# Attention scores as float32 products in four row groups of packed keys, in place of two bfloat16 products over split operands

## The chip, the cores and the metric

The kernel runs on one core of one Trainium2 chip. The metric is the time of one launch in microseconds of the device (us); the lower the better. Engines: TensorE (PE: matmuls, PEld: loading of its stationary operand), VectorE (DVE), ScalarE (ACT), GpSimd (POOL) and SyncE (SP, which only issues DMAs).

## What is computed

Four blocks act on x of (2 images, 32 channels, 64 x 64 pixels) in float32, each as x = x + block(normalised x). Three are convolutions: two deformable 3x3 convolutions with a 1x1 one between them. The fourth is attention over the N = 4096 pixels of each image, and the change is there:

```
f1 = einsum('oc,bcn->bon', w1, g) + b1      # queries, 32 channels
f2 = einsum('oc,bcn->bon', w2, g) + b2      # keys
f3 = einsum('oc,bcn->bon', w3, g) + b3      # values
A  = softmax(einsum('bcn,bcm->bnm', f1, f2), axis=-1)
x  = x + (einsum('bcm,bnm->bcn', f3, A) + g)      # g: x normalised for each channel
```

## The kernel before, in words

Every engine has its own program of instructions, executed in the order in which they are written; semaphores order the engines among each other. There is no scheduler: the order in the source is the order on the chip. So an instruction that waits holds up all that is queued behind it on its engine.

The last convolution samples by four corners. Image 0 is finished first: a part of it by products of whole bands of rows (`dense_and_tiles`), the rest, like all of image 1, by tiles of 128 pixels, whose corners POOL fetches with nine indirect DMAs a tile (L499) into four slots. A slot is free when the tile four before it has been sampled. For one tile VectorE weights the corners (L818) and adds them (L828, L832), TensorE turns the samples (`turn`, L1656), ScalarE copies them out (`tile`, L1337), TensorE multiplies them by the weights (`convolve`, L1664), and VectorE adds the result to x (`finish`, L853). Image 1 has 32 tiles: eight go through in `pairs(1, ...)`, between the band work and attention, in four pairs with attention's preparation beside them; the other 24 go through beside the attention of image 0, four in each of its first six blocks (the merged blocks).

Attention goes over 8 blocks of 512 queries for each image (`attend`), and for each block over 16 pairs of 128 keys (step s). Three things are done for a block:

- **Maxima of the next block.** 32 products of 128 queries by 512 keys from the high bfloat16 parts alone (`score_chunks`, L1808, "chunks"), written to two PSUM banks in turn; VectorE takes each one's maximum along the row (`largest`, L1085). Chunk c may be written when the maximum of chunk c-2 has been taken. At the block's end the maxima are negated, split in three bfloat16 parts (`negated`, L1092 to L1101), turned on TensorE (`turn_maxima`, L1816) and copied into a row (`maxima_row`, L1109).
- **Scores.** Queries and keys stand as three bfloat16 parts (high, middle, low). A pair of key tiles takes two products of 128 rows (L1851) and two of 67 rows, which hold the rest and the maxima's row (L1855). They go to two of four banks, so that ScalarE's exponential (L1455, 1024 wide) of one pair runs beside the next pair's scores.
- **Weighted sums.** Values times probabilities (`weigh`, L1826) in float32, two products of 64 columns in one bank. ScalarE copies the block's sums out (L1447), VectorE adds both halves, divides and adds to x (`sum_part` k = 0 to 6).

Ahead of it, for each image: projections (`project`, L1762) in float32, ScalarE's high parts (L1409, L1410), VectorE's remainders (`split`, L1031 to L1034), 32 turns of the values (L1782) and twelve DMAs by SP that spread the parts over the partitions (`spread_a`, `spread_b`). For image 1 all of this stands in the last two blocks of image 0 (`prepare_image_1`). The number of chunks in each step, and the steps of the sum's parts, come from tables:

```
CHUNKS = [2] * 8 + [3] * 4 + [2] * 2 + [0] * 2
MERGED_CHUNKS = [2, 2, 3, 3, 1, 2, 3, 3, 1, 2, 3, 3, 2, 2, 0, 0]
LAST_CHUNKS = [0] * 7 + [4] * 8 + [0]
```

In a merged block a tile takes four steps: its corners are weighted at s % 4 == 0, summed at s % 4 == 1, turned at the end of s % 4 == 2 and convolved at the end of s % 4 == 3.

## Time and profile before

| | |
|---|---|
| median of 3 runs | 1409.59 us (1409.26 to 1412.25) |
| the profiled execution | 1411.1 us, of which its span is 1409.0 us |
| busy, share of the span | TensorE 85%, VectorE 73%, ScalarE 45%, GpSimd 38% |
| chain that ended last | TensorE 62%, VectorE 22%, issue 8%, DMA 3%, ScalarE 2% |
| TensorE's granted clock, mean | 0.927 of full |

The stages by time (us from the span's start): up to 250 the first convolution, to 300 the 1x1 one, to 601 the second convolution's bands with the tiles of image 0, 601 to 691 `pairs(1, ...)`, 691 to 969 the six merged blocks, 969 to 1085 the two blocks in which image 1 is prepared, 1085 to 1398 image 1's attention, then its last sum and the store.

Busy times of engines are read beside each other within one stage. A row of the timeline gives a start, a duration, an engine, a line of the kernel and the tiles written and read; a count "x4" means that so many instructions in a row were merged. A float32 product is recorded as two instructions.

### The profile page before, as it was taken

What the parts mean: (1) busy time and instruction counts of PE and PEld (TensorE: products, weight loads), DVE (VectorE), ACT (ScalarE), POOL (GpSimd) and SP (SyncE); (2) the same over time, 40 slices, a digit from 0 to 9 for tenths busy, and PEclk for the clock granted to TensorE, in tenths of its full rate; (3) what the DMA queues carried; (4) which work ended last, traced back from release to release, by engine and by line L of the source; (5) the groups of instructions that cost most, each with busy time, mean ns of one, the idle gap of its engine ahead of it and who ended that gap; (6) DMA issues with size and microseconds to landing.
All of it is one profiled execution on the core that took longest, in us unless ns stands there. A gap on an engine that the chain in (4) does not pass through costs nothing.

```text
span 1409.0 us, 18575 instructions
## 1 busy us (share of the span) xinstructions
PE 1201.2 (85%) x6192; PEld 484.6 (34%) x6253; DVE 1031.7 (73%) x1727; ACT 636.5 (45%) x772; POOL 541.7 (38%) x530
## 2 busy tenths in 40 slices
PE   3688883287999999965799999998888999999996
PEld 0466662042444444322233333332222222222221
DVE  5399998874866666576779888988757677777771
ACT  2666665345455545240144444344562444444443
POOL 8000000247787877776777777760000000000000
PEclk9899997598999999955699999999998999999998
DMA  1455540047433352115111111110021000000000
GB/s 42 105 121 115 123 106 1 0 136 248 147 112 114 113 151 73 49 53 129 51 51 51 51 50 52 50 41 0 0 60 31 15 0 1 0 0 0 0 0 15
DMA packets 59201, 86.58 MB, mean 61 GB/s; under 512 B 12358, under 2 KB 39494, under 8 KB 58246
## 3 DMA queue, kind: packets, MB, share of 16 engines
q1 hardware_dynamic: 44166, 55.09, 15.1%
q0 software_dynamic: 14976, 30.70, 7.7%
q8 instruction: 37, 0.61, 0.2%
q14 instruction: 22, 0.18, 0.0%
HBM read 72.12 MB, written 7.34 MB: 56 GB/s over the span
## 4 chain that ended last, share of the span: by engine, by line
PE 62%; DVE 22%; issue 8%; DMA 3%; ACT 2%; DVEq 1%; SPq 1%; another core or an unknown queue 1%; ACTq 0%
PE psum L1692 16%; PE psum L1826 14%; PE psum L1808 8%; PE psum L1851 6%; PE psum L1855 6%; DVE maxes L1085 4%; PE psum L1664 3%; DVE products_or_attention L699 3%; PE psum L1702 2%; DVE probs_and_weighted L699 2%; PE psum L1529 2%; DVE probs_and_weighted L828 1%; PE psum L1656 1%; DVE quads L341 1%; DVE probs_and_weighted L818 1%
## 5 line engine op out<-in xcount | busy, mean ns | idle before, releaser
L499 POOL DMA_INDIRECT tile_data<-quad_table,index_u x468 | 493.2, 1054 | 160.8 <-issue 142.0
L1085 DVE TENSOR_REDUCE maxes<-psum 128x1 f32<-128x512 f32 x512 | 337.9, 683 | 128.9 <-PE psum L1808 113.8
L1455 ACT ACTIVATE probs_and_weighted<-psum 128x1024 f32<-128x1024 f32 x256 | 262.1, 1024 | 355.9 <-PE psum L1855 355.6
L1826 PE MATMUL psum<-probs_and_weighted,quads 128*64 128x512 f32 x1024 | 280.6, 627 | 0.5
L1692 PE MATMUL psum<-scratch,quad_rows_or_splits 128*128 128x512 f32 x486 | 227.5, 609 | 12.6 <-DVE scratch L914 12.6
L1855 PE MATMUL psum<-products_or_attention 67*128 (+1 forms) x512 | 155.2, 384 | 1.1 <-DVE products_or_attention L1109 1.1
L1692 PEld LDWEIGHTS psum<-scratch,quad_rows_or_splits 128*128 128x128 f32 x486 | 88.1, 192 | 125.9 <-issue 125.9
L341 POOL TENSOR_SCALAR quads<-x_state,norm 32x4096 f32<-32x4096 f32 x6 | 34.1, 5679 | 235.7 <-DVE norm L583 234.9
L925 DVE TENSOR_TENSOR probs_and_weighted<-psum,quads 128x512 f32<-128x512 f32 x81 | 55.3, 687 | 90.6 <-PE psum L1692 85.0
L1808 PE MATMUL psum<-products_or_attention 128*128 128x512 bf16 x250 | 101.9, 419 | 17.8 <-DVE maxes L1085 15.0
L1581 PE MATMUL psum<-quad_rows_or_splits 64*128 64x128 f32 x1152 | 83.6, 288 | 26.3 <-DVE products_or_attention L699 18.2
L1808 PE MATMUL psum<-tile_data 128*128 128x512 bf16 x246 | 91.1, 392 | 6.7 <-DMA tile_data<-quad_rows_or_splits 4.6
L1337 ACT ACTIVATE vals<-psum 96x384 f32<-96x384 f32 x52 | 25.3, 486 | 140.7 <-PE psum L1656 140.7
L1826 PEld LDWEIGHTS psum<-probs_and_weighted,quads 128*64 128x64 f32 x1024 | 51.2, 136 | 103.2 <-issue 100.0
L1581 PEld LDWEIGHTS psum<-quad_rows_or_splits 64*128 64x128 f32 x1152 | 72.6, 193 | 39.4 <-ACT quad_rows_or_splits L1304 22.7
L1363 ACT ACTIVATE quads<-quads,band_columns 128x512 f32<-128x512 f32 x81 | 52.5, 711 | 65.6 <-DVE probs_and_weighted L925 65.6
L1851 PE MATMUL psum<-tile_data 128*128 (+1 forms) x236 | 72.9, 384 | 7.4 <-DMA products_or_attention<-quad_rows_or_splits 4.7
L1851 PE MATMUL psum<-products_or_attention 128*128 (+1 forms) x231 | 72.6, 388 | 4.0 <-issue 4.0
L1855 PEld LDWEIGHTS psum<-products_or_attention 67*128 67x128 bf16 x512 | 50.7, 99 | 63.8 <-issue 2.8
L818 DVE TENSOR_TENSOR probs_and_weighted<-tile_data 128x1152 f32<-128x1152 f32 x52 | 70.3, 1351 | 0.0
L1529 PE MATMUL psum<-quads,off_w 128*32 128x512 f32 x256 | 33.3, 666 | 41.4 <-DVE quads L341 41.4
L1808 PEld LDWEIGHTS psum<-products_or_attention 128*128 (+1 forms) x256 | 23.5, 97 | 123.8 <-DVE maxes L1085 61.5
(204 smaller groups left out, 1402.6 us busy)
## 6 DMA issues: line engine op xcount, KB each, us to landing
products_or_attention<-positions SPq DMA_DIRECT2D x32, 576.0 KB, 8.3
products_or_attention<-bands SPq DMA_DIRECT2D x18, 768.0 KB, 9.9
tile_data<-quad_table,index_u POOLq DMA_INDIRECT x468, 2.5
quads<-bands SPq DMA_DIRECT2D x9, 768.0 KB, 9.3
products_or_attention<-quad_rows_or_splits SPq DMA_DIRECT2D x16, 256.0 KB, 5.7
quad_table<-quad_rows_or_splits SPq DMA_DIRECT2D x4, 768.0 KB, 9.5
tile_data<-quad_rows_or_splits SPq DMA_DIRECT2D x8, 256.0 KB, 5.1
quad_table<-quad_rows_or_splits SPq DMA_DIRECT2D x2, 640.0 KB, 8.7
```

The costliest lines, as they stand in the source:

```text
L499: pool.indirect_dma_start(out=out[:, k * CORNERS * C:(k + 1) * CORNERS * C], out_offset=None, in_=table, in_offset=bass.IndirectOffsetOnAx ...
L699: v.tensor_tensor(out4, psum[:, mix_bank(b, ky), 0:TAP3].rearrange("p (k j c) -> p k j c", k=3, c=C), corner_w[:, rows_at(at), 3 * ROWS4 * ...
L818: v.tensor_tensor(weighted[:, :].rearrange("p (q k c) -> p k q c", q=CORNERS, c=C), corners_of.rearrange("p (k q c) -> p k q c", k=TAPS, q ...
L1085: v.reduce_max(maxes[:, c // NBLK, c % NBLK:c % NBLK + 1], psum[:, FREE + c % 2, :], AXIS_X)\
L1455: act.activation(probs[:, s % 2, :], psum[:, SCORES + 2 * (s % 2):SCORES + 2 * (s % 2) + 2, :] .rearrange("p a n -> p (a n)"), ACT.Exp).th ...
L1529: pe.matmul(psum[C * g:C * g + C, bank, :].rearrange("p (y x) -> p y x", x=W), off_w_sb[d][:, s, :], grid[:, y:y + 8, sx:sx + W], start=s ...
L1581: last = pe.matmul(psum[:, mix_bank(b, ky), P * kx:P * kx + P], hat_x[rows, n % 2, 3 * ky + kx, :], img_t[rows, (2 * n + ky) * C:(2 * n + ...
L1692: last = pe.matmul(psum[:, m, :], band_img[:, j, 4 * C * m:4 * C * (m + 1)], band_sel[:, n % 2, j, :], start=j == 0, stop=j == BAND_PAIRS - 1)
L1808: pe.matmul(psum[:, FREE + c % 2, :], qa[b][:, tile_of_q], ka[b][:, BLK * (c % NBLK):BLK * (c % NBLK) + BLK], start=True, stop=True)\
L1826: last = pe.matmul(psum[2 * C * h:2 * C * h + 2 * C, SUMS, :], f3[b][:, 2 * s + h, :], probs[:, s % 2, BLK * h:BLK * h + BLK], start=s == ...
L1851: pe.matmul(dst[h], ka[b][:, keys[h]], qa[b][:, here], start=True, stop=False)
L1855: done = pe.matmul(dst[h], kb[0:rows_b, keys[h]], qb[0:rows_b, here], start=False, stop=True)
```

## The change

- **Scores.** Keys are packed: partitions 32r to 32r+31 of `keys` hold the keys of tile 4m+r, in float32. A step now covers four key tiles (8 steps a block, `KEY_QUADS`): four float32 products of 32 rows, one for each row group, each into its own bank, then four bfloat16 products of 3 rows that add the maxima. The block's queries stand four times below each other in `q_now`, which VectorE copies from `q_rep` for each block (`take_queries`). All four banks serve one step: a step's scores wait for both exponentials of the step before.
- **Preparation** by "fills" of one bank each: 8 of keys and 8 of queries for the maxima (float32 products of 33 rows by 128 columns, of which VectorE and ScalarE keep high part and rest in one bfloat16 array), 2 of packed keys, 2 of values (16 small products each). No parts in a third split, no turns of values, no DMAs. Image 0's 20 fills stand in `pairs(1, ...)`: 13, 2, 3 and 2. Image 1's first 14 stand in the last two blocks of image 0, the other six one to a block in image 1's own blocks.
- **Chunks** keep their form, their number (32 a block) and their two banks. In a step they stand in three places: after the scores, between the two halves of the weighted sums, and after them.
- **Tiles in a merged block** take two steps: in an even step weighted before the step's maxima, summed after them and turned at the step's end, in the odd one convolved.
- **Sums.** ScalarE copies both halves apart (two instructions for one); VectorE's own copy (L1117) goes.

```diff
-KEY_PAIRS = TILES // 2
+KEY_QUADS = TILES // 4
-CHUNKS = [2] * 8 + [3] * 4 + [2] * 2 + [0] * 2
-MERGED_CHUNKS = [2, 2, 3, 3, 1, 2, 3, 3, 1, 2, 3, 3, 2, 2, 0, 0]
-LAST_CHUNKS = [0] * 7 + [4] * 8 + [0]
+SCORED = [4, 5, 5, 5, 5, 4, 4, 0]
+MERGED_SCORED = [3, 6, 3, 6, 3, 6, 5, 0]
+LAST_SCORED = [0, 0, 0, 8, 8, 8, 8, 0]
...
 # VectorE, attend
-                for s in range(KEY_PAIRS):
...
+                for s in range(KEY_QUADS):
                     if prepare is not None:
                         prepare(s)
+                    if tiles and s % 2 == 0 and s:
+                        finish(1, *merged_pair(j, s // 2 - 1))
+                    if tiles and s % 2 == 0:
+                        weight_corners(1, *merged_pair(j, s // 2))
+                    largest(b_next, nxt, range(c, c + scored_at[s]))
+                    c += scored_at[s]
+                    if tiles and s % 2 == 0:
+                        sum_corners(1, *merged_pair(j, s // 2))
+                    if s == KEY_QUADS - 1 and more:
+                        take_queries(b_next, nxt)
                         negated(b_next, nxt)
+                    if s and not first:
+                        sum_part(b, prev, s - 1)
+                    if ahead and s == 3:
+                        read_fill(1, fill_ahead(j), (var, stp, start + 2))
...
 # VectorE, beside the pairs of tiles
-            pairs(1, [[l3_normed, l3_split],
-                         [lambda: largest(0, first, range(0, 8))],
-                         [lambda: largest(0, first, range(8, 20))],
-                         [lambda: largest(0, first, range(20, CHUNK_N)), lambda: negated(0, first),
-                          lambda: maxima_row(0, first)]])
+            pairs(1, [[l3_normed, lambda: fills(*range(13))],
+                      [lambda: largest(0, first, range(0, 8)), lambda: fills(13, 14)],
+                      [lambda: largest(0, first, range(8, 20)), lambda: fills(15, 16, 17)],
+                      [lambda: largest(0, first, range(20, MAXIMA)), lambda: fills(18, 19), lambda: take_queries(0, first),
+                       lambda: negated(0, first), lambda: maxima_row(0, first)]])
...
 # ScalarE, a fill
+                act.wait_ge(filled, lin(fills, 1, 1))
+                if kind == "q":
+                    act.activation(q_rep[b][:, here], bank, ACT.Identity)
+                act.activation((qa if kind == "q" else ka)[b][:, here], bank, ACT.Identity).then_inc(high_taken, 1)
...
 # TensorE, a fill
+                if kind in "qk":
+                    last = pe.matmul(psum[:, bank, :], w_rep[:, 0 if kind == "q" else 1, :, :].rearrange("p r c -> p (r c)"),
+                                     g2[0:C + 1, here], start=True, stop=True)
...
+                    for t in range(16):
+                        lo = P * (16 * at + t)
+                        last = pe.matmul(psum[:, bank, C * t:C * t + C], g2[0:C + 1, lo:lo + P], w123_sb[:, 2 * C:3 * C],
+                                         start=True, stop=True)
...
 # TensorE, attend
+                for s in range(KEY_QUADS):
+                    wait(pe, probs_ready, lin(n, 2))
+                    if s == 0:
+                        pe.wait_ge(q_ready, lin((var, stp, start + NBLK * b), 1, 1))
+                    for i in range(4):
+                        mine = slice(C * i, C * i + C)
+                        pe.matmul(psum[:, SCORES + i, :], keys[b][mine, P * s:P * s + P], q_now[mine, :],
+                                  start=True, stop=False)
                     if s == 0:
                         pe.wait_ge(nm_rows, lin((var, stp, start + NBLK * b), 1, 1))
+                    for i in range(4):
+                        mine = slice(C * i, C * i + SPLITS)
+                        done = pe.matmul(psum[:, SCORES + i, :], ones_h[mine, :], nm_row[mine, :], start=False, stop=True)
...
+                    cuts = [c, c + min(m, 2), c + max(min(m, 2), m // 2 + min(m, 2) // 2), c + m]
+                    score_chunks(b_next, nxt, range(cuts[0], cuts[1]))
+                    for half in range(2):
+                        if weighing:
+                            weigh(*earlier, half)
+                        score_chunks(b_next, nxt, range(cuts[1 + half], cuts[2 + half]))
                     c += m
+                    if tiles and s % 2 == 0:
+                        turn(1, *merged_pair(j, s // 2))
+                    if tiles and s % 2 == 1:
+                        convolve(1, *merged_pair(j, s // 2))
                     if prepare is not None:
                         prepare(s)
```

How the change moves TensorE's work in a merged block (the loop over blocks 1 to 5, its start). Before, up to and past the first tile's turn; L1851 and L1855 are scores, L1808 a chunk, L1826 a weighted sum, L1656 the turn:

```order
L1855 MATMUL psum<-products_or_attention 128x512 x2
L279 REGISTER_ALU
L1808 MATMUL psum<-products_or_attention 128x512
L1824 REGISTER_ALU
L1826 MATMUL psum<-probs_and_weighted,quads 64x512 x2
L279 REGISTER_ALU
L1808 MATMUL psum<-products_or_attention 128x512
L279 REGISTER_ALU
L1808 MATMUL psum<-products_or_attention 128x512
L1653 ISA
L279 REGISTER_ALU
L1656 MATMUL psum<-ident,sampled 96x128 x3
```

Now, in the first (even) step, behind its four scores (L1893) and the maxima's four products (L1899); L1852 is a chunk, L1870 a weighted sum, L1690 the turn:

```order
L276 ISA
L1852 ISA
L1852 MATMUL psum<-products_or_attention 128x512
L276 REGISTER_ALU
L1852 MATMUL psum<-products_or_attention 128x512
L1867 REGISTER_ALU
L1870 MATMUL psum<-quads 64x512 x4
L276 REGISTER_ALU
L1852 MATMUL psum<-products_or_attention 128x512
L1687 ISA
L276 REGISTER_ALU
L1690 MATMUL psum<-ident,sampled 96x128 x3
```

The turn stood in the third of four steps; it stands now at the end of the step in which its tile is weighted and summed. VectorE has for that same even step (L830 weights, L840 and L844 sum, L1092 are maxima):

```order
L830 TENSOR_TENSOR probs_and_weighted<-tile_data 128x9x4x32
L1091 ISA
L1092 TENSOR_REDUCE maxes<-psum 128x1
L1091 REGISTER_ALU
L1092 TENSOR_REDUCE maxes<-psum 128x1
L1091 REGISTER_ALU
L1092 TENSOR_REDUCE maxes<-psum 128x1
L838 ISA
L840 TENSOR_TENSOR probs_and_weighted<-probs_and_weighted 128x576
L842 REGISTER_ALU
L276 REGISTER_ALU
L844 TENSOR_TENSOR sampled<-probs_and_weighted 128x288
```

Three maxima stand between the weighting and the sums, and the third is that of the chunk behind all four weighted sums in TensorE's piece.

TensorE beside the first pairs of tiles of image 1, before and then now (the fills are L1808, L1812 and L1819 now; L1762 and L1782 are projections and turns before):

```order
L1762 MATMUL psum<-conv_sums_or_normed,w_sb 96x512 x8
L1782 MATMUL psum<-ident,quad_rows_or_splits 128x32 x32
L1656 MATMUL psum<-ident,sampled 96x128 x3
L1664 MATMUL psum<-vals,conv_w 32x128 x3
L1656 MATMUL psum<-ident,sampled 96x128 x3
L1664 MATMUL psum<-vals,conv_w 32x128 x3
L1808 MATMUL psum<-products_or_attention 128x512 x8
```

```order
L1808 MATMUL psum<-conv_sums_or_normed,w_rep 128x512 x9
L1812 MATMUL psum<-conv_sums_or_normed,w_sb 32x512 x8
L1819 MATMUL psum<-w_sb,conv_sums_or_normed 128x32 x32
L1690 MATMUL psum<-ident,sampled 96x128 x3
L1698 MATMUL psum<-vals,conv_w 32x128 x3
L1690 MATMUL psum<-ident,sampled 96x128 x3
L1698 MATMUL psum<-vals,conv_w 32x128 x3
L1852 MATMUL psum<-products_or_attention 128x512 x8
L1808 MATMUL psum<-conv_sums_or_normed,w_rep 128x512 x2
```

Seven more fills (L1808 now: two, three and two) stand behind the chunks of the three pairs that follow, where before only chunks stood.

## Rows read from the trace of the kernel before

**Rows 1.** Stages: per engine busy us (x instructions), then granted clock, DMA share, GB/s

```profile
613.50:627.40 13.90, 13.85 (x16) 4.32 (x16) 9.96 (x17) 8.24 (x14) 10.58 (x11) 0.50 0.16 47
...
735.50:969.00 233.50, 219.27 (x980) 74.65 (x1000) 203.28 (x340) 94.88 (x106) 159.39 (x161) 1.00 0.16 45
```

**Rows 2.** Timeline of VectorE: the copy of the maxima's row that opens a block

```profile
691.11 0.69 DVE L1109 CAST products_or_attention<-psum 3x512 bf16<-3x512 f32 x1 [0.68 <-PE psum L1816]
...
735.52 0.69 DVE L1109 CAST products_or_attention<-psum 3x512 bf16<-3x512 f32 x1 [0.68 <-PE psum L1816]
...
969.32 0.69 DVE L1109 CAST products_or_attention<-psum 3x512 f32 x1 [0.59 <-PE psum L1816]
...
1085.12 0.69 DVE L1109 CAST products_or_attention<-psum 3x512 bf16<-3x512 f32 x1 [0.48 <-PE psum L1816]
...
1130.56 0.69 DVE L1109 CAST products_or_attention<-psum 3x512 bf16<-3x512 f32 x1 [1.22 <-PE psum L1816]
...
1364.26 0.69 DVE L1109 CAST products_or_attention<-psum 3x512 f32 x1 [1.33 <-PE psum L1816]
```

**Rows 3.** Timeline of one step in a block of image 1

```profile
1203.52 0.38 PE L1808 MATMUL psum<-tile_data 128*128 128x512 bf16 x1
1203.71 1.02 ACT L1455 ACTIVATE probs_and_weighted<-psum 128x1024 f32<-128x1024 f32 x1 [1.39 <-PE psum L1855]
...
1203.83 1.08 PE L1826 MATMUL psum<-probs_and_weighted,quads 128*64 128x512 f32 x4
1203.93 0.69 DVE L1085 TENSOR_REDUCE maxes<-psum 128x1 f32<-128x512 f32 x1 [0.39 <-PE psum L1808]
...
1204.84 0.39 PE L1808 MATMUL psum<-tile_data 128*128 128x512 bf16 x1
```

**Rows 4.** Timeline of TensorE: float32 products of 32 and of 64 rows

```profile
259.59 3.22 PE L1756 MATMUL psum<-quad_rows_or_splits,l_sb 32*32 32x512 f32 x32
...
149.71 1.40 PE L1581 MATMUL psum<-quad_rows_or_splits 64*128 64x128 f32 x22
```

**Rows 5.** Timeline beside the first pairs of image 1: TensorE, ScalarE, VectorE's split

```profile
613.55 13.97 PE L1762 MATMUL psum<-conv_sums_or_normed,w_sb 33*96 33x512 f32 x16 [2.98 <-DVE conv_sums_or_normed L1022]
627.45 1.91 PE L1782 MATMUL psum<-ident,quad_rows_or_splits 32*128 32x32 f32 x16
...
645.89 0.63 PE L1808 MATMUL psum<-products_or_attention 128*128 128x512 bf16 x1 [1.42 <-DMA products_or_attention<-quad_rows_or_splits]
...
615.67 0.59 ACT L1409 ACTIVATE quad_rows_or_splits<-psum 64x512 bf16<-64x512 f32 x1 [5.03 <-PE psum L1762]
...
626.33 0.68 DVE L1031 TENSOR_TENSOR scratch<-psum,quad_rows_or_splits 64x512 f32<-64x512 f32 x1
```

**Rows 6.** Timeline of a merged block: a tile on VectorE, its turn and products on TensorE

```profile
751.54 0.34 DVE L853 SCALAR_TENSOR_TENSOR x_state<-psum,columns,x_state 32x128 f32 x1
...
751.99 1.35 DVE L818 TENSOR_TENSOR probs_and_weighted<-tile_data 128x1152 f32<-128x1152 f32 x1
...
754.95 0.75 DVE L828 TENSOR_TENSOR probs_and_weighted<-probs_and_weighted 128x576 f32<-128x576 f32 x1
755.73 0.47 DVE L832 TENSOR_TENSOR sampled<-probs_and_weighted 128x288 f32<-128x288 f32 x1
...
745.35 0.49 PE L1656 MATMUL psum<-ident,sampled 128*96 128x128 f32 x3
...
748.74 0.84 PE L1664 MATMUL psum<-vals,conv_w 96*32 96x128 f32 x6
```

**Rows 7.** Source view of the gathers: durations ns, first and last start

```profile
L499 POOL DMA_INDIRECT tile_data<-quad_table,index_u x468: 940/944/3170, 304.3 to 942.7; - x156
```

**Rows 8.** Timeline of ScalarE: the copy of the last block's sums

```profile
1398.09 0.60 ACT L1447 ACTIVATE scratch<-psum 128x512 f32<-128x512 f32 x1 [1.24 <-PE psum L1826]
```

**Rows 9.** Stages around a fall of the clock, columns as in rows 1

```profile
1001.00:1004.50 3.50, 2.04 (x7) 0.45 (x6) 3.17 (x6) 0.19 (x1) 0.00 (x0) 1.00 0.02 5
1004.50:1008.50 4.00, 3.88 (x10) 0.96 (x11) 0.69 (x1) 2.20 (x3) 0.00 (x0) 0.57 0.00 0
```

More of the change, by code:

```diff
@@ L265, in build @@
         N_CONST = 16 * (9 * DEFORMS + 11)
[L266 to L267 removed]
+        NM_STEPS, SUM_STEPS = 5, 6
         def lin(n, scale=1, off=0):
@@ L1843, in attend @@
[L1843 to L1851 removed]
+                    b_next, nxt = 1, (0, 0, 0)
@@ L1852, in attend @@
                     if s == 0:
                         pe.wait_ge(nm_rows, lin((var, stp, start + NBLK * b), 1, 1))
-                    for h in range(2):
-                        done = pe.matmul(dst[h], kb[0:rows_b, keys[h]], qb[0:rows_b, here], start=False, stop=True)
-                    done.then_inc(scored, 1)
-                    if s == KEY_PAIRS - 1 and more and not last:
-                        turn_maxima(b, nxt)
-                    m = chunks[s]
-                    ahead = min(m, max(1, m // 2))
```

518 lines of the change are left out of this document (260 added, 258 removed).

## The prediction

> **What bounds the kernel now.** I read the stages first [rows 1], then VectorE's timeline for the copies that open the blocks [rows 2], then single steps. Before attention TensorE runs at half its clock (granted 0.50, 1.2 GHz), although it is busy without a gap [rows 1, 5]. In the merged blocks the clock is full, TensorE is busy 219.27 of 233.5 us and VectorE 203.28: both near a bound, five blocks of 46.7 us [rows 1, 2]. The first merged block takes 44.4 (735.52 less 691.11). The two blocks behind them take 115.8 together, four of image 1 and a fifth run from 1130.56 to 1364.26 with two more, that is six of 38.95 [rows 2]. There a step is TensorE alone: two bfloat16 products cost 0.43, a pair of weighted sums 1.32 from one chunk's start to the next, of which 0.215 is the chunk and 1.107 the sums with the changes of tiling [rows 3]. 64 bfloat16 products for scores, 32 chunks and 16 pairs make 13.8 + 6.9 + 17.7 = 38.4, plus some 0.5 for other things: a saving in scores counts in full there, and only there.
>
> **The scores.** Four pairs of products cost 8 x 0.215 = 1.72 for four key tiles. Now there are four float32 products of 32 rows. Before, such products in four row groups ran together: 16 of 512 columns (32 instructions) in 3.22 us, so 0.81 for four, where one by one each instruction at 0.43 would make 13.8 [rows 4]. A float32 pass of 512 columns at full clock is 0.43 (half of 0.87, [rows 5]), so I take 0.86; the four bfloat16 products of the maxima together 0.215; 0.30 for two changes of row groups and a load that nothing covers (a pair of sums shows 0.25 for its own). That is 1.38 for 1.72. Bounds: 1.07 with nothing exposed, 1.6 with the four loads one after another, 3.5 + 0.9 if the groups don't run together. A step saves 0.34, a block 2.7.
>
> The Trainium skill ("TensorE: Matmul & The Clock Gate", on LDWEIGHTS) has a load of 32 rows cost as much as one of 128, which speaks against the change. If four of these stood one after another in each of the 128 steps, an estimate of 0.2 us a step adds 26 us. The 22 instructions of 64 rows in 1.40 us, loads included, speak against that [rows 4].
>
> **Image 0's preparation: +23.** Before: eight projections in 13.97 us and 64 small instructions of 0.12 (1.91 for 16), 7.6 us, up to 634.5; VectorE's split, two of 0.68 and a shorter one for each projection, ran along [rows 5]. Now the first 13 fills are eleven of 1.75 (13.97 / 8) and two of 7.6 / 2: 26.9, and 640.3 instead of 634. One TensorE wait for the spreading DMAs goes, 1.42 [rows 5], so the chunks start 4.8 later. Seven fills more stand behind the chunks of the next three pairs. Each is 1.75 on TensorE, and the last of each group keeps the pair waiting for ScalarE's two copies of 0.59 [rows 5] and VectorE's 0.69, since the next pair's work is queued behind it: 2 x 1.75 + 1.9 = 5.3, 3 x 1.75 + 1.4 = 6.6, then 5.4. The sum is 22.1, with the four-fold `take_queries` 23. With the clock at full instead it would be 9; nothing here lets it rise, since the engine was busy throughout and stayed at 0.50 [rows 1]. Attention starts at 714.5.
>
> **Merged blocks: +33.** VectorE must do for a tile: index and weights 0.17 and 1.35, sums 0.75 + 0.47, `finish` 0.34 [rows 6], nine maxima of 0.69 [rows 3] and two parts of the sums, 0.9 each by what the stage's total leaves for them: 11.1 us in two steps. It does them in this order in an even step: finish, weights, three maxima, sums. TensorE (from 0): scores to 1.4, two chunks, four weighted sums with their changes, third chunk at 3.9. VectorE starts that maximum 0.41 later, is done at 5.0, sums to 6.35, and the turn waits for it: TensorE stands about 2.4 us, turns (0.49, [rows 6]) and ends the step at 6.84. Before, the tile was summed a whole step ahead of its turn. The odd step has 1.4 + 6 x 0.215 + 2.5 + 0.84 for the products of the tile [rows 6] = 6.05, and scores of the next can't be moved forward, because everything on TensorE is in order. A pair of steps is 12.9, a block of four 13.2 + 12.9 + 12.9 + 13.4 = 52.4 (the ends hold the block's negation, split and row, 0.3 and 0.5 more). Against 46.7: +5.7, five times 28.5; the first, which has no sums to write, +5. The gathers don't bind: the last one starts at 942.7 for a stage that ends at 969 [rows 7, 2], and slower blocks give them more time. Break-even is a block of 46.1 with the head's later start left aside: a wait of 0.8 or less.
>
> **Blocks 6 and 7 of image 0: -13.** They take 115.8, where two merged blocks took 93.4, for image 1's preparation [rows 2]. It loses VectorE's three-part splits (about 1.8 a projection, now 0.69 a fill), a memset of a whole row, turns and DMAs. I put the first, which waited most for splits, at 46.5, as a merged block of before, and the second, with most of the fills at half clock, at 56. Bounds -22 (two blocks of 46.7) and +5 (13 half-clock fills of 1.75 in line, no wait saved): it is the least known term.
>
> **Image 1: -6.** Block 0 +0.5; blocks 1 to 5 save 2.7 and 0.2 of chunks' waits give back, and one query fill of 33 rows adds 1.1 and leaves about 38.25 for 38.95: -3.5; block 6 has no wait for a fill, 37.3: -1.5. The last block has no chunks to hide in: scores, both exponentials of 1.02 [rows 3], next scores go round in 1.4 + 0.4 (a product's end to ScalarE's start) + 2 x 1.02 - 0.1 = 3.75, eight times 30 with 2.1 ahead and behind, for 33.8 of before [rows 2, 8]: -1.7; its tail +0.2. Double-banked scores ran beside the exponentials; with four banks a step's scores wait for both of the step before. With chunks and sums between (4.4 of a step's 4.8) this hides; in the last block it shows. Bounds -20 (1.07 a step) and +20 (1.6 a step).
>
> ScalarE's second copy of the sums is hidden (it is busy 41% of a merged block, 94.88 of 233.5 [rows 1]; were that gone it would cost 0.5 a block).
>
> **The sum.** 23 + 33 - 13 - 6 = +37 us on the profiled execution's 1411.1: 1448. The median of the runs stands 1.5 below that execution, so 1447.
>
> **Rivals.**
> - *TensorE isn't left waiting (faster).* If a merged block is held by VectorE's own work or by the gathers alone, one takes 42.6 (the six before had 44 to 46.7, VectorE busy 87%) to 45. What goes for it: In the new order its maxima come in three places, closer to their chunks, so the third may be early. Against: the third maximum waits for a product that is written behind four sums. Six blocks save 3 to 4 each, 22 in all: 23 - 22 - 13 - 6 = -18, up to -22: 1389 to 1393 on the execution, 1389 for the median. It decides when the turn's wait is under 0.8.
> - *The two cancel.* Half of the wait: 1410 to 1418.
> - *The clock falls in the merged blocks.* After stretches with TensorE busy 2.04 of 3.5 us the next 4 us were granted 0.57 [rows 9]: 1.7 us lost. Even steps now have a wait of 2.4. With half of 23 of them followed by such a stretch 19 to 25 us: 1467 to 1473. The six merged blocks of before, with waits under 1.5, were at 1.00 [rows 1]. The Trainium skill (the same page, on the clock gate) says that idle time puts the array back to half clock; the rows of 1004.5 agree.
> - *The loads of four row groups stand one after another:* +0.2 a step, 1470.
> - *The row groups don't run together,* 4 x 0.86 and 4 x 0.215 for 1.07: +3.2 for 128 steps less what waits hide, some 1790. Rows 4 speak against it.
>
> **How the numbers follow.** Main course 0.50, clock falls 0.17, loads in line 0.05, groups in line 0.02: slower 0.74. Faster 0.20; the cancelling case 0.06 splits into 0.05 within 0.2% (2.8 us, about what a measurement here can tell) and 0.01 faster. The main case's own range, by the bounds of blocks 6 and 7, of image 1 and of the wait (1.5 to 3), is 1425 to 1470. For 8 in 10 I take 1392 to 1485: outside lie half of the faster rival, the groups in line and the worst of the clock.
>
> **What would show it.** VectorE's copy of the first maxima's row near 714; copies 52 apart in merged blocks; before the turn in an even step TensorE idle 2.4 with `sampled` as releaser; steps of 1.38 for scores; blocks of image 1 38.2 apart. Wrong would be: copies 43 to 46 apart, scores of over 1.7, or TensorE's clock at 1.00 from 614 on.

## The result, and the profile after

The changed kernel takes **1475.15 us** (median of 4 runs, 1474.4 to 1476.14) against 1409.59: 1.0468 times the time of before, interval 1.0454 to 1.0481. The profiled execution took 1476.14 us, its span is 1474.3, 65.3 more than before. TensorE's mean granted clock fell from 0.927 to 0.895. All medians are of fast executions: one slow one of sums_first (1888.31 us) and one of values_32 (2339.33) are left out.

VectorE's copy of the maxima's row opens each block, as in [rows 2]. In the timeline of the changed kernel (start, duration, engine, line, operation):

```profile
720.03 0.69 DVE L1119 CAST nm_row<-psum 128x512 bf16<-128x512 f32 x1 [0.71 <-PE psum L1859]
...
774.99 0.69 DVE L1119 CAST nm_row<-psum 128x512 bf16<-128x512 f32 x1 [1.27 <-PE psum L1859]
...
830.46 0.69 DVE L1119 CAST nm_row<-psum 128x512 bf16<-128x512 f32 x1 [0.37 <-PE psum L1859]
...
1058.23 0.69 DVE L1119 CAST nm_row<-psum 128x512 bf16<-128x512 f32 x1 [0.58 <-PE psum L1859]
...
1164.17 0.69 DVE L1119 CAST nm_row<-psum 128x512 bf16<-128x512 f32 x1 [2.24 <-PE psum L1859]
```

From these starts and those of [rows 2] the whole difference can be told by stage:

| stage | before, us | after, us | difference | forecast |
|---|---|---|---|---|
| up to image 0's attention | 691.1 | 720.0 | +28.9 | +23 |
| six merged blocks | 278.2 | 338.2 | **+60.0** | +33 |
| blocks 6 and 7 of image 0 | 115.8 | 105.9 | -9.9 | -13 |
| image 1 and the store | 323.9 | 310.1 | -13.8 | -6 |
| sum | 1409.0 | 1474.3 | +65.3 | +37 |

**Merged blocks.** Timeline of an even step (weigh-up of a tile on VectorE L830, maxima L1092, sums L840 and L844; on TensorE chunk L1852, turn L1690, next scores L1893 and L1899):

```profile
832.17 1.94 PE L1870 MATMUL psum<-quads 128*64 128x512 f32 x8
...
832.53 1.42 DVE L830 TENSOR_TENSOR probs_and_weighted<-tile_data 128x1152 f32<-128x1152 f32 x1
...
833.98 1.89 DVE L1092 TENSOR_REDUCE maxes<-psum 128x1 f32<-128x512 f32 x3
...
834.73 0.39 PE L1852 MATMUL psum<-products_or_attention 128*128 128x512 bf16 x1 [0.61 <-DVE maxes L1092]
...
836.65 0.46 DVE L844 TENSOR_TENSOR sampled<-probs_and_weighted 128x288 f32<-128x288 f32 x1
...
837.24 0.53 PE L1690 MATMUL psum<-ident,sampled 128*96 128x128 f32 x3 [2.12 <-DVE sampled L844]
...
837.70 1.94 PE L1893 MATMUL psum<-quads,probs_and_weighted 32*128 32x512 f32 x8
...
839.40 0.67 PE L1899 MATMUL psum<-nm_row,ones_h 3*128 3x512 bf16 x4
```

TensorE has its chunk done at 835.1 and stands 2.12 us until the samples are summed. Then its scores take 1.70 us (837.70 to 839.40), where they take 0.96 at full clock (below). The same piece by stretches (us, busy time of PE, PEld, DVE, ACT, POOL with instructions, then granted clock, DMA share, GB/s):

```profile
834.00:837.20 3.20, 0.50 (x3) 0.10 (x1) 2.99 (x5) 1.18 (x2) 2.59 (x3) 1.00 0.21 61
837.20:841.20 4.00, 3.96 (x19) 1.21 (x21) 0.55 (x1) 1.61 (x3) 2.87 (x4) 0.59 0.16 49
```

That is the pattern of [rows 9] in the merged blocks, which were at 1.00 before [rows 1] and are at 0.83 to 0.91 now. Waits of the six blocks (us, times, longest):

```profile
PE psum L1690 <- DVE sampled L844: 50.0, 24, 2.3
```

24 tiles, 24 waits, of 1.9 to 2.3 us each. Before, the same wait is 4.9 us in 6 times. Not every wait is followed by a fall: through these six blocks the granted clock goes down 17 times, each time within 2 us of the end of one of the 24 waits, or in it.

**Image 1.** Timeline of TensorE in one step of it, beside [rows 3]:

```profile
1251.52 1.14 PE L1893 MATMUL psum<-quads,probs_and_weighted 32*128 32x512 f32 x8
1252.48 0.40 PE L1899 MATMUL psum<-nm_row,ones_h 3*128 3x512 bf16 x4
1252.81 0.60 PE L1852 MATMUL psum<-quad_rows_or_splits,tile_data 128*128 128x512 bf16 x2
```

Four key tiles' scores take 1252.81 - 1251.52 = 1.29 us, 1.72 before. Blocks are 37.8 apart (1209.30, 1247.14, 1284.95), 38.9 before.

**Ahead of attention.** Timeline of TensorE beside the first pairs of image 1, to be read beside [rows 5]:

```profile
614.22 15.72 PE L1808 MATMUL psum<-conv_sums_or_normed,w_rep 33*128 33x512 f32 x18 [2.98 <-DVE conv_sums_or_normed L1037]
...
633.44 13.86 PE L1819 MATMUL psum<-w_sb,conv_sums_or_normed 33*128 33x32 f32 x64
...
657.52 1.03 PE L1852 MATMUL psum<-products_or_attention 128*128 128x512 bf16 x2
```

The 13 fills end at 647.3; the chunks start at 657.5, 11.6 later than before. And TensorE's clock, back at 694 before (three us into attention), now comes back twelve us into it:

```profile
720.00:732.00 12.00, 9.41 (x36) 2.39 (x36) 7.54 (x12) 4.36 (x5) 5.54 (x6) 0.50 0.11 33
732.00:734.00 2.00, 2.00 (x9) 0.32 (x7) 1.13 (x2) 0.00 (x0) 1.40 (x2) 0.98 0.16 45
```

### The profile page after: what moved, and what is told of

Same layout as the page of the kernel before. It is cut to its first block, busy times and chain, and to the rows that moved or that the text cites. A ratio compares the mean times of both kernels' runs of the same rounds, so it can differ in the third digit from the quotient of the medians.

```text
span 1474.3 us, 19666 instructions
## 1 busy us (share of the span) xinstructions
PE 1228.8 (83%) x6893; PEld 481.0 (33%) x6893; DVE 1018.6 (69%) x1712; ACT 638.9 (43%) x804; POOL 539.6 (37%) x534
## 4 chain that ended last, share of the span: by engine, by line
PE 63%; DVE 21%; issue 9%; ACT 2%; DMA 2%; DVEq 1%; SPq 0%; ACTq 0%
PE psum L1726 15%; PE psum L1870 14%; PE psum L1852 9%; PE psum L1893 8%; DVE maxes L1092 4%; PE psum L1808 3%; DVE products_or_attention L711 2%; PE psum L1698 2%; PE psum L1690 2%; PE psum L1736 2%; PE psum L1899 2%; PE psum L1563 2%; DVE probs_and_weighted L711 2%; PE psum L1819 2%; DVE probs_and_weighted L840 1%
## 5 line engine op out<-in xcount | busy, mean ns | idle before, releaser
L1092 DVE TENSOR_REDUCE maxes<-psum 128x1 f32<-128x512 f32 x512 | 330.2, 684 | 164.4 <-PE psum L1852 161.2
L1488 ACT ACTIVATE quads<-psum 128x1024 f32<-128x1024 f32 x256 | 248.0, 1020 | 324.6 <-PE psum L1899 308.3
L1870 PE MATMUL psum<-quads 128*64 128x512 f32 x1024 | 280.8, 644 | 0.0
L1893 PE MATMUL psum<-quads,probs_and_weighted 32*128 32x512 f32 x1024 | 160.3, 698 | 2.3 <-ACT quads L1488 1.5
L1852 PE MATMUL psum<-products_or_attention 128*128 128x512 bf16 x256 | 98.6, 451 | 14.7 <-DVE maxes L1092 13.9
L1852 PE MATMUL psum<-quad_rows_or_splits,tile_data 128*128 128x512 bf16 x256 | 85.5, 391 | 13.8 <-DVE maxes L1092 13.2
L1870 PEld LDWEIGHTS psum<-quads 128*64 128x64 f32 x1024 | 57.1, 141 | 118.0 <-issue 114.9
L1690 PE MATMUL psum<-ident,sampled 128*96 128x128 f32 x156 | 31.4, 318 | 71.1 <-DVE sampled L844 69.0
L830 DVE TENSOR_TENSOR probs_and_weighted<-tile_data 128x1152 f32<-128x1152 f32 x52 | 70.4, 1353 | 0.0
L1852 PEld LDWEIGHTS psum<-products_or_attention 128*128 (+1 forms) x256 | 19.1, 100 | 145.3 <-DVE maxes L1092 100.1
L1852 PEld LDWEIGHTS psum<-quad_rows_or_splits,tile_data 128*128 (+1 forms) x256 | 17.8, 97 | 137.8 <-DVE maxes L1092 118.5
L926 DVE SCALAR_TENSOR_TENSOR scratch<-products_or_attention,band_columns 128x512 f32<-128x512 f32 x81 | 55.6, 735 | 7.5 <-ACT products_or_attention L1389 7.5
```

Of the source, the lines that this page charges most:

```text
L830: v.tensor_tensor(weighted[:, :].rearrange("p (q k c) -> p k q c", q=CORNERS, c=C), corners_of.rearrange("p (k q c) -> p k q c", k=TAPS, q ...
L1092: v.reduce_max(maxes[:, c // NBLK, c % NBLK:c % NBLK + 1], psum[:, FREE + c % 2, :], AXIS_X)\
L1488: act.activation(probs[:, s % 2, 2 * BLK * h:2 * BLK * (h + 1)], psum[:, SCORES + 2 * h:SCORES + 2 * h + 2, :].rearrange("p a n -> p (a n) ...
L1690: last = pe.transpose(psum[0:3 * C, SAMPLES, P * g:P * g + P], sampled[:, u, 3 * C * g:3 * C * g + 3 * C], ident[:, :])
L1852: pe.matmul(psum[:, FREE + c % 2, :], qa[b][:, tile_of_q], ka[b][:, lo:lo + BLK], start=True, stop=True).then_inc(chunk_scored, 1)
L1870: last = pe.matmul(psum[2 * C * h:2 * C * h + 2 * C, SUMS, :], f3[b][:, 4 * s + i, :], probs[:, s % 2, BLK * i:BLK * i + BLK], start=s == ...
```

## The experiments

Theory L: in the merged blocks TensorE is left waiting for the samples, and its clock falls behind that wait. Rivals: VectorE's load or the gathers hold these blocks in any order (V); the clock falls for another reason (C). All times are medians; where a run is set beside the kernel before, that is the one measured with it (1408.8 to 1410.2).

### sums_first: VectorE sums the tile ahead of the maxima

```diff
                         weight_corners(1, *merged_pair(j, s // 2))
+                        sum_corners(1, *merged_pair(j, s // 2))
                     largest(b_next, nxt, range(c, c + scored_at[s]))
                     c += scored_at[s]
-                    if tiles and s % 2 == 0:
-                        sum_corners(1, *merged_pair(j, s // 2))
```

> The changed kernel, with the tile's sums ahead of the step's three maxima on VectorE (TensorE's program untouched). Theory L (lock-step: TensorE is left waiting for the samples, and the clock falls behind that wait): the wait ahead of the turn falls from 2.1 to under 0.3 us, the granted clock of the merged blocks from 0.83 to 0.91 back to 1.00, a merged block takes 45 to 47 instead of 55 to 60, and the time is 1410 to 1420. Rival V (VectorE's load or the gathers hold the merged blocks, whatever the order): blocks stay over 53, time over 1465. Rival C (the clock falls for another reason than that wait): the wait goes but the clock stays near 0.88, time 1430 to 1445.

Measured: **1419.0 us**, 56 less than the changed kernel and in the range of theory L. No wait for samples is left, later merged blocks are 48.3 apart (813.43, 861.74, 910.01), where L had 45 to 47. V falls. The clock came back to 0.96, not 1.00: a new wait stands in the place of the old, in every even step. The view of waits of 720 to 1000 (us, times, longest), then the timeline of a block's first even step:

```profile
PE psum L1851 <- DVE maxes L1092: 38.7, 24, 2.3
...
817.78 0.46 DVE L844 TENSOR_TENSOR sampled<-probs_and_weighted 128x288 f32<-128x288 f32 x1
...
818.27 1.89 DVE L1092 TENSOR_REDUCE maxes<-psum 128x1 f32<-128x512 f32 x3
819.02 0.39 PE L1851 MATMUL psum<-products_or_attention 128*128 128x512 bf16 x1 [1.94 <-DVE maxes L1092]
...
819.67 1.59 PE L1892 MATMUL psum<-quads,probs_and_weighted 32*128 32x512 f32 x8
```

The third chunk needs the bank of the first, whose maximum now stands behind the sums: 1.94 us, and the scores behind it are slow again (1.35 to the next instruction's start at 821.02, for 0.96). There are 24 such waits, of 1.3 to 2.3 us, and the clock falls at only 4 of them (once in each of four blocks, each time at a wait of 1.9 us or more); at the others it stays at 1.00.

### warm_wait: TensorE kept busy in the same wait

```diff
                     if tiles and s % 2 == 0:
+                        wait(pe, outs_read, lin(tile_no(1, *merged_pair(j, s // 2))))
+                        for _ in range(9):
+                            pe.matmul(psum[:, SAMPLES, :], ones_h[:, :], ka[b][:, 0:BLK],
+                                      start=True, stop=True)
                         turn(1, *merged_pair(j, s // 2))
```

> The changed kernel, with nine bfloat16 products of 128x512 that nobody reads (9 x 0.215 = 1.9 us) ahead of each turn in a merged block, where TensorE waits for the samples anyway. Theory L: TensorE is busy through the wait, so the clock stays at 1.00, and what is left is the wait alone: a block of 52 to 53, time 1446 to 1454; the difference to the changed kernel (21 to 29 us) is the price of the clock. Rival C: the clock stays at 0.88, time 1475 or more. Rival V: 1475, since TensorE's speed doesn't matter.

Measured: **1441.15 us**, 34.0 less than the changed kernel, by adding 216 products. Theory L had the way of it but not the size: 1446 to 1454, with 21 to 29 us for the clock. Timeline of TensorE, then a stretch of merged blocks (columns as above):

```profile
838.05 2.11 PE L1922 MATMUL psum<-products_or_attention,ones_h 128*128 128x512 bf16 x9
840.18 0.53 PE L1690 MATMUL psum<-ident,sampled 128*96 128x128 f32 x3
840.64 1.14 PE L1893 MATMUL psum<-quads,probs_and_weighted 32*128 32x512 f32 x8
841.60 0.40 PE L1899 MATMUL psum<-nm_row,ones_h 3*128 3x512 bf16 x4
```

```profile
775.00:830.00 55.00, 51.82 (x290) 17.79 (x292) 42.42 (x72) 19.82 (x25) 41.72 (x41) 1.00 0.18 49
```

The scores are back to 0.96, the clock to 1.00, blocks are 50.65 apart (821.12, 871.78, 922.44). Rival C falls: it is that wait. The merged stage takes 304.3 (719.38 to 1023.69). So of its +60.0 us, 33.9 are the clock behind the wait, and 26.1 the rest. That rest is the wait above all: 45.1 us more of it than before (50.0 for 4.9), less what the scores save, 48 steps of 0.43 (1.72 less 1.29), 20.6.

### turn_odd: the turn a step later, VectorE's order left alone

```diff
 # TensorE
                     score_chunks(b_next, nxt, range(cuts[0], cuts[1]))
+                    if tiles and s % 2 == 1:
+                        turn(1, *merged_pair(j, s // 2))
...
-                    if tiles and s % 2 == 0:
-                        turn(1, *merged_pair(j, s // 2))
 # ScalarE
-                    if tiles and s % 2 == 0:
+                    if tiles and s % 2 == 1:
                         tile(1, *merged_pair(j, s // 2))
```

> The changed kernel with VectorE's order left as it is; TensorE turns the tile in the odd step, behind that step's scores and first two chunks, ScalarE copies it behind that step's exponentials. Theory L (only the distance from the sums to the turn counts): the samples are there about when TensorE comes to them, the wait is under 0.5 us, the clock is back, blocks of 46 to 48, time 1412 to 1422, as with sums_first. Rival (VectorE's order of work is what matters, the maxima ahead of the sums): time over 1440.

Measured: **1403.91 us**, 71 less than the changed kernel and 0.9971 of the kernel before (0.9958 to 0.9983): the changed kernel with one thing in another place beats it, by 0.3%. It is 8 us better than the best that theory L had (1412 to 1422, blocks of 46 to 48), and the rival, over 1440, falls. Merged blocks are 44.7 apart (809.35, 854.07, 898.77). Timeline of TensorE, and a stretch:

```profile
816.08 0.53 PE L1690 MATMUL psum<-ident,sampled 128*96 128x128 f32 x3 [0.30 <-DVE sampled L844]
```

```profile
811.00:857.00 46.00, 42.26 (x239) 13.25 (x240) 41.16 (x71) 19.46 (x24) 35.60 (x34) 1.00 0.17 48
```

The turn now has a step's scores and two chunks between it and the place where it stood. That takes most of the wait: of 720 to 1000, 7.7 us in 11 times are left, the longest 1.0, and the clock doesn't fall. That it does better than sums_first because the weights and the sums stand apart again on VectorE, and so hold no chunk for long, fits the waits for maxima (13.2 us for 38.7), but wasn't tested by itself. VectorE is busy 89%.

### even_two: two chunks in even steps, seven in odd ones

```diff
-MERGED_SCORED = [3, 6, 3, 6, 3, 6, 5, 0]
+MERGED_SCORED = [2, 7, 2, 7, 2, 7, 5, 0]
```

with the edit of sums_first.

> As sums_first (1419.0), and an even step has two chunks instead of three, an odd one seven instead of six, so none stands behind the weighted sums in an even step. In sums_first TensorE still waits up to 1.94 us there, for the bank that VectorE frees late, once in each block of 48.2 us, and the clock falls behind it (0.96). Theory L: that wait and the half clock go, blocks of 45 to 46, time 1402 to 1408. Rival V (VectorE's 11.2 us of work for two steps is now the bound, so it doesn't matter where the chunks stand): blocks stay at 48, time 1418 to 1420.

Measured: **1417.1 us**, 2 less than sums_first. By the time that is below rival V's range by a hair, and far from theory L's. But neither holds as stated: blocks are 47.4 apart, and VectorE is busy 86% of one (40.7 us), so it isn't the bound:

```profile
811.00:857.00 46.00, 40.55 (x226) 12.72 (x223) 39.60 (x65) 18.00 (x22) 35.94 (x34) 0.96 0.17 47
```

The expectation had read sums_first wrongly, with one wait a block where there are four. Here the timeline has waits at the first turn of the block for the samples, in an odd step for a bank, and the longest, once in a block, in its last even step, which still has five chunks:

```profile
816.19 0.53 PE L1689 MATMUL psum<-ident,sampled 128*96 128x128 f32 x3 [1.29 <-DVE sampled L844]
...
822.30 0.39 PE L1851 MATMUL psum<-products_or_attention 128*128 128x512 bf16 x1 [0.65 <-DVE maxes L1092]
...
850.53 0.39 PE L1851 MATMUL psum<-products_or_attention 128*128 128x512 bf16 x1 [1.89 <-DVE maxes L1092]
```

Behind this last one the clock falls (at 851.1, and again behind the same wait of the next two blocks): that is the 0.96.

### fills_first and dense_fills: image 0's fills

fills_first has `fills(*range(FILLS))` in the first pair on VectorE, ScalarE and TensorE, and no fills in the three others. dense_fills adds to it:

```diff
                                      g2[0:C + 1, here], start=True, stop=True)
+                    if b == 0:
+                        for _ in range(2):
+                            pe.matmul(psum[:, FREE, :].rearrange("p (a n) -> p a n", a=4), ones_h[:, :],
+                                      ones_h[:, None, :].to_broadcast([P, 4, P]), start=True, stop=True)
```

> The changed kernel, with all 20 fills of image 0 ahead of the first chunks, in the first pair, none behind the chunks. In the changed kernel the seven late fills keep the pairs for 4.9 + 6.6 + 4.9 = 16.4 us. Theory (each group of late fills pays the way through ScalarE and VectorE once more): seven fills in line cost 7 x 1.75 = 12.2, so 4 us less, 1471. Rival (only TensorE's time counts): no difference, 1475.

Measured: **1468.0 us**, 7 less, where the theory had 4; attention starts at 714.6 instead of 720.0. Not all of it is the fills. In the profiled executions 2.2 us are there before the first fill (611.99 for 614.22), where both kernels do the same, and 3.2 lie in the merged blocks (335.0 for 338.2), for which no cause is shown. What is left for the fills is 3.2: the direct way for seven of them (12.29 us in one piece) is cheaper than three trips through ScalarE and VectorE, by about what was expected.

> As fills_first (1468.0), with two bfloat16 products of 128 rows by 512 columns that nobody reads behind each of the 16 fills of keys and queries of image 0. There TensorE is busy for 45 us without a gap in products of 33 rows and the clock stays at 0.50. Theory R (the clock stays low because only 33 of 128 rows are used, not because TensorE idles): products of all rows in between bring it to 1.00; a fill with its two then takes 1.3 instead of 1.75, values go at full clock, 10 to 20 us less in all, 1448 to 1458. Rival I (it is something else, such as what ran before): the clock stays at 0.50 and each fill takes 0.86 longer: 14 us more, 1482.

Measured: **1488.24 us**, 20 more than fills_first. A fill with its two products takes 2.97 us, 1.03 of it the two, instead of 1.75. TensorE is busy without a gap, a third of it with products of all rows, and stays at half clock:

```profile
625.00:640.00 15.00, 15.00 (x31) 3.24 (x34) 3.74 (x5) 3.47 (x6) 5.53 (x6) 0.50 0.11 31
```

Rival I, of these two.

### combined and turn_and_fills

combined is even_two with fills_first, turn_and_fills is turn_odd with fills_first.

> even_two and fills_first together. If their savings add (7 us for the fills, 12 to 17 for the chunks on the 1419.0 of sums_first): 1396 to 1401, below the 1409.4 of the kernel before. If even_two saves nothing beyond sums_first: 1412.

Measured: **1413.97 us**, 3 less than even_two, near the second of the two cases. Attention starts 3.5 earlier than in even_two (716.18 for 719.66) and the span ends 3.3 earlier (1412.2 for 1415.5). So what the fills save is kept; but it is 3.5 us and not 7, and even_two saves 2 of the 12 to 17.

> turn_odd (1403.9) and fills_first (7 us less than the changed kernel) together. If the two savings add, as they stand in different stages: 1397 to 1400, 9 to 12 below the kernel before. Rival (as with combined, where the earlier start was given back in the merged blocks): 1402 to 1404.

Measured: **1403.81 us**, the same as turn_odd, as the rival has it; 0.9957 of before (0.9941 to 0.9973). Attention starts 3.6 earlier (716.91 for 720.55) and four blocks go as in turn_odd, 43.9 to 44.8. Then two take 46.8 and 46.7. The timeline of VectorE shows why:

```profile
908.62 0.17 DVE L853 CAST index_u<-index_f 128x9 uint32 x1 [0.86 <-DMA tile_data<-quad_table,index_u]
```

It waits for the gathers, by the view of waits of 895 to 988 six times (us, times, longest):

```profile
DVE index_u L853 <- DMA tile_data<-quad_table,index_u: 3.6, 6, 0.9
```

And POOL issues them without a pause, each 0.30 us behind the end of the last. But first it had stood still for 31.47 us, until a slot was free:

```profile
665.27 1.46 POOL L511 DMA_INDIRECT tile_data<-quad_table,index_u  x1 [31.47 <-DVE sampled L844]
...
905.99 0.94 POOL L511 DMA_INDIRECT tile_data<-quad_table,index_u  x1 [0.30 <-issue]
907.24 0.94 POOL L511 DMA_INDIRECT tile_data<-quad_table,index_u  x1 [0.30 <-issue]
```

36 times 1.25 is 45 us a block; with those that take longer it is 48.2 (737.6 to 930.5 for four times 36), more than 44.7. So the gathers live on the lead that they have when attention starts, and it is used up before the stage ends. The lead is smaller here than in turn_odd, where POOL stood 16.9 and 5.2 us for a slot: with all 20 fills in the first pair, the next tiles are sampled later. What the preparation saves is given back here (988.49 for 988.17 at the stage's end). It isn't what held combined back, although the expectation says so: that one kept its earlier start.

### burst: 24 products of all rows ahead of the fills

```diff
+                for _ in range(24):
+                    pe.matmul(psum[:, FREE, :].rearrange("p (a n) -> p a n", a=4), ones_h[:, :],
+                              ones_h[:, None, :].to_broadcast([P, 4, P]), start=True, stop=True)
                 pe.wait_ge(g3_ready, 1)
```

> As turn_and_fills, with 24 bfloat16 products of 128 rows by 512 columns that nobody reads, in one piece, ahead of the fills (10 us at half clock, part of it in a wait of 3 us). Theory B (a piece of work with all rows and without a gap brings the clock back, as it came back shortly after attention's start): the clock is 1.00 through the fills, a fill of keys takes 0.87 instead of 1.75, the 45 us of fills become 23, attention starts 8 to 16 us earlier, time 1382 to 1392. Rival S (the clock stays at 0.50 there whatever TensorE does, as with dense_fills): attention starts 7 us later, 1404 to 1407.

Measured: **1405.39 us**, as rival S has it, but the profile shows neither theory: attention starts at 715.76, 1.2 us earlier than in turn_and_fills, and not 7 later or 8 to 16 earlier. And the time could not have told them apart: the last merged block takes 46.7 as there, with the gathers behind, so an earlier start was given back in any case. Timeline of TensorE, and the stretches:

```profile
609.41 7.62 PE L1830 MATMUL psum<-ones_h 128*128 128x512 bf16 x24
616.96 11.91 PE L1808 MATMUL psum<-conv_sums_or_normed,w_rep 33*128 33x512 f32 x18
```

```profile
609.40:613.40 4.00, 4.00 (x11) 1.49 (x11) 2.76 (x4) 0.14 (x1) 3.52 (x2) 0.50 0.12 33
613.40:617.00 3.60, 3.60 (x17) 1.37 (x14) 0.00 (x0) 0.00 (x0) 2.83 (x3) 0.91 0.21 59
617.00:620.00 3.00, 3.00 (x8) 1.37 (x8) 1.14 (x2) 1.36 (x3) 2.12 (x3) 1.00 0.15 44
620.00:623.00 3.00, 3.00 (x6) 1.35 (x5) 2.14 (x4) 1.63 (x3) 2.39 (x3) 0.64 0.21 64
623.00:632.00 9.00, 9.00 (x23) 2.28 (x22) 4.14 (x6) 2.88 (x5) 6.84 (x8) 0.50 0.19 51
```

The burst brought the clock to 1.00; it fell again inside the fills, while TensorE was busy 3.00 of 3.00 us with float32 products of 33 rows. What the first nine fills gained (11.91 us for 15.72) the burst had nearly cost: they start at 616.96, 2.7 later than in turn_and_fills.

### values_32, split_values and one_group

values_32 has `g2[0:C, lo:lo + P]` and `w123_sb[0:C, 2 * C:3 * C]` in the values' fills; the values' bias is left out.

> The changed kernel, with the values' products over 32 rows instead of 33: the values' bias is left out. In the changed kernel 64 such instructions take 13.86 us (0.217 each), where 0.119 was forecast from products of 32 rows. Theory (33 rows reach into a second row group, so the next load waits): 0.12 each for 32 rows, 6 us less for image 0 and, at full clock, about 3 less for image 1: time 1466 to 1470. Rival (the load from these data costs 0.217 at half clock whatever the rows): unchanged, 1475.

Measured: **1475.97 us**, the rival. The line's own row is unchanged to the digit:

```profile
631.56 13.86 PE L1819 MATMUL psum<-w_sb,conv_sums_or_normed 32*128 32x32 f32 x64
```

split_values is turn_odd with each of image 1's fills of values in two halves:

```diff
-                    fill(1, n)
+                    fill(1, n, part=(8, 16) if fill_kind(n)[0] == "v" else (0, 16))
...
                         score_chunks(b_next, nxt, range(cuts[1 + half], cuts[2 + half]))
+                        if prepare is not None and half == 0:
+                            values_half(j[2], s)
```

> As turn_odd (1403.9), with each of image 1's two fills of values in two halves of eight products, one between the weighted sums of the step and one at its end. In the changed kernel TensorE is busy 4.00 of 4 us in such a fill (32 small instructions of 33 rows, 4.5 us) and the clock falls to 0.50 at its end, and stays there for 4 and for 7 us of the following work. Theory R (the clock falls on work that uses few rows, when it is long enough, even without a gap): with 2.2 us at a time and products of all rows between, it stays at 1.00, the block of 60.7 takes 55 to 57, time 1398 to 1400. Rival I (the clock falls only on idle time, here the waits for maxima ahead of the fill): falls stay, time 1403 to 1405.

Measured: **1403.52 us**, no gain, the time of rival I. The second of image 0's two blocks takes 61.9 (1031.43 to 1093.33, 60.7 in turn_odd) and the clock falls behind the first half already. In the timeline the half takes 1.90 us to the next start and the weighted sums behind it 1.95 instead of 1.08:

```profile
1064.69 1.97 PE L1819 MATMUL psum<-w_sb,conv_sums_or_normed 33*128 33x32 f32 x16
1066.59 1.95 PE L1876 MATMUL psum<-quads 128*64 128x512 f32 x4
```

This doesn't show rival I: TensorE waits 0.56 us for a maximum ahead of the half, as it does in other steps, behind which the clock stays at 1.00. Theory R is wrong about how short a piece does no harm; which of the two brings the clock down isn't told apart here.

one_group puts all four score products, and the maxima's four, in the first row group, so that scores are of other keys:

```diff
-                        mine = slice(C * i, C * i + C)
+                        mine = slice(0, C)
...
-                        mine = slice(C * i, C * i + SPLITS)
+                        mine = slice(0, SPLITS)
```

> The changed kernel with the four score products of a step and the maxima's four all in the first row group: the same number and size of products, but on the keys of the first tile of four alone, so other scores. Theory G (the four row groups run at the same time): without it a step costs 4 x 0.86 + 4 x 0.215 = 4.3 us instead of 1.29, so 3.0 x 128 steps, less what the waits of the merged blocks hide: 1475 + 330 to 385 = 1805 to 1860. Rival (the products run one after another in the changed kernel too, only faster than reckoned): 1475 to 1500.

Measured: **2210.38 us**. The row groups do run at the same time in the changed kernel. The size was at least 350 us off: the four products cost what theory G has (3.54 us, at a granted clock of 1.00), but the clock falls too, to 0.761 over the whole run. How much of the 350 that makes wasn't taken apart. Timeline and one stretch of image 1:

```profile
2001.61 3.69 PE L1893 MATMUL psum<-quads,probs_and_weighted 32*128 32x512 f32 x8
2005.15 1.02 PE L1899 MATMUL psum<-nm_row,ones_h 3*128 3x512 bf16 x4
```

```profile
2100.00:2200.00 100.00, 99.52 (x212) 29.73 (x210) 11.63 (x21) 20.94 (x23) 0.00 (x0) 0.64 0.00 0
```

3.54 us for the four products where four groups take 0.96. In the stretch TensorE is busy 99.52 of 100 us and is granted 0.64.

## Why the prediction was right, and where it wasn't

The direction and the reason held: slower, because the turn waits for samples in its own step. The time was 28 us above the forecast (1475 for 1447), inside the range. That range is wide (1392 to 1485, with the time of before in it), and that the time lies in it is partly luck: the slow clock alone cost 33.9 us, and the result stays below 1485 thanks to image 1 (7.8 better than forecast) and to a shorter wait and shorter scores in the merged blocks (6.9 better). The whole is 5.9 for image 0's preparation, 33.9 less 6.9 for the merged blocks, 3.1 for blocks 6 and 7, less 7.8 for image 1: 28.2. By its steps:

- **The scores**: 1.29 us a step, forecast 1.38 from [rows 3, 4]. The bound of 1.6 with the loads one after another is out, and with it the estimate of 26 us: the eight loads of a step overlap, together they have 0.31 us recorded, and nothing waits for them. The Trainium skill ("TensorE: Matmul & The Clock Gate", LDWEIGHTS) states the price of one load, the same for 32 rows as for 128; no run here compares the two, and that the loads would stand in line was the prediction's own assumption.
- **Merged blocks, the wait**: forecast a turn's wait of 2.4 and blocks of 52.4; measured 1.9 to 2.3, and 50.65 with the clock at full. Term of +33, shown as +26.
- **Merged blocks, the clock**: here it failed. The term for it in the sum was nothing. The text held apart, as a rival with a chance of 0.17, what comes with the same mechanism: each even step has a wait of two us, and behind such waits the clock falls. The stretches of [rows 9] had shown the pattern. The rival took half of 23 waits at 1.7 us, 19 to 25 us; the trace has 17 falls behind 24 waits, and warm_wait's 33.9 us make about 2 us for each.
- **The rival on the other side** (TensorE not left waiting, 1389) is not what the changed kernel does, but turn_odd makes its condition true and gives 1404. By stages, the head is 6 us later than that rival had it, the merged blocks save 10.6 (267.6 for 278.2) and not 22, and image 1 makes up 8. Blocks of 42.6 weren't to be had from the supply either: the gathers are spaced 1.25 us at the least, 45 us a block, where the prediction has 42.6 to 45 for blocks held by the gathers alone. Its own count of VectorE's work, 11.1 us for two steps, makes 44.4 a block too, and 39.9 were measured.
- **Image 0's preparation**: +28.9 for +23. The mis-sized term is the values: 64 instructions at 0.119 from turns of the same shape [rows 5] made 7.6 us, and 13.86 were measured, 6.3 more. The rows were also misread: before, the 32 turns are 32 instructions in two halves of 1.9 us with 3.2 us of waiting between them, not 64 in 7.6. One turn (`pe.transpose`) is one instruction, one product two, so a product costs 0.434 where a turn cost 0.119. The 33rd row isn't the cause (values_32). Why a single instruction takes 0.217 for 0.119, both at half clock, is left open. The seven late fills cost 17.3 with the queries' copy (28.9 less 11.6), for 18 in the forecast.
- **Blocks 6 and 7**: -9.9 for -13, inside its bounds: 44.9 and 61.1 us for 46.5 and 56. The miss is the second, which has most of the fills and a half clock behind those of the values.
- **Image 1**: -13.8 for -6. Five blocks of 37.8 (38.25), the one before the last 36.0 (37.3), and the last block, 28.9 us up to the copy of its sums for 32.1: a round of scores and two exponentials is 3.44 us and not 3.75. Both exponentials together take 1.94 and ScalarE idles 1.50 for the scores in between, where I had 1.94 and 1.8. In its timeline:

```profile
1442.51 1.94 ACT L1488 ACTIVATE quads<-psum 128x1024 f32<-128x1024 f32 x2 [1.50 <-PE psum L1899]
```

## What to carry to other kernels

When an order written out by hand is made coarser (eight steps for sixteen), check for each product of one engine how much of the other engines' work stands between it and its use: here one turn moved behind the next step's scores and two chunks is worth 71 of 1475 us. A wait of two us on TensorE is to be priced with the slow stretch that may stand behind it: here 17 of 24 had one, and they cost more (34 us) than the rest of the stage's loss (26). And before a stage is made faster, look which supply is next, and how large its lead is (here the gathers, 48 us a block where a block takes 44.7).

## What the runs showed of the hardware

- **The clock isn't told by busy time.** The Trainium skill ("TensorE: Matmul & The Clock Gate", on the HAM clock gate) has activity release the throttle and idleness bring it back. The waits here agree (0.59 behind a wait of 2.1 us, 1.00 with the wait filled), though not one for one: 17 falls behind 24 waits of 1.9 to 2.3 us, 4 behind 24 of 1.3 to 2.3 in sums_first. But the clock also fell on a TensorE that was busy all the time: in burst from 1.00 to 0.50 inside float32 products of 33 rows, and in one_group to 0.64 over 100 us with products of 32 rows in one group. In the changed kernel the same number of 32-row products in four groups together runs at 1.00. In dense_fills, busy without a gap and with products of all rows for 1.03 of each 2.97 us, it stayed at 0.50. What exactly counts was not settled; split_values, made on the idea that short pieces of few rows do no harm, failed.
- **Doing nothing useful was faster than waiting**: 216 more products, 34 us less.
- **Four 32-row float32 products in four row groups take 0.96 us, in one group 3.54**, both at a granted clock of 1.00; the maxima's four take 0.40 and 1.02.
